# State-space output with channels on partitions, and decay exponents from four shared products with rows spread by small DMAs

## What is computed

```python
scores = einsum('bic,bjc->bij', q, q); out = softmax(scores) @ v * gamma + inputs        # attention over 1024 tokens
t = layernorm(out)                                                                      # then a state-space layer
dt = softplus(dt + dt_bias); dA = exp(dt * -exp(A_log))                                 # 8 heads
state = state * dA_t + (dt_t * x_t) * B_t;  y = einsum('bhpn,bn->bhp', state, C_t)      # 8 heads x 32 channels, 32 states
y = rmsnorm((y + Dp * xs) * silu(z), gnorm_w, 1e-05);  t = t + x + y @ W_out.T
logits = layernorm(t) @ router_w.T                                                      # then 8 experts, the best 2 per token
```

## Time and profile before

| | |
|---|---|
| median of 3 runs | 1214.97 us (1214.96 to 1219.69) |
| span of the profiled execution | 1181.1 us |
| median minus span | 33.9 us |
| busy share of the span: PE, DVE, ACT, POOL | 92%, 72%, 64%, 53% |
| mean granted TensorE clock | 0.970 |

### The profile page before, as it was taken

One profiled execution on the slowest core, in us unless ns is written; L12 is line 12 of the kernel. 1 busy time (PEld: TensorE's weight loads), 2 busy tenths in 40 slices (PEclk: granted clock), 3 DMA queues, 4 the chain that ended last, 5 costly groups with the idle time before them and its releaser, 6 DMA issues.

```text
span 1181.1 us, 29643 instructions
## 1 busy us (share of the span) xinstructions
PE 1083.7 (92%) x8432; PEld 998.3 (85%) x8433; DVE 852.1 (72%) x3071; ACT 754.7 (64%) x1903; POOL 624.9 (53%) x981
## 2 busy tenths in 40 slices
PE   3889999999999999999999999867889999999993
PEld 2779888888988988988888888856789999999883
DVE  3488888988988888888898898776355644444564
ACT  1567777777767777767777777742476666666551
POOL 8122444467557566556646655743744665444442
PEclk9999999999999999999999999976799999999997
DMA  7200000001000100100100000010122222223666
GB/s 221 61 1 28 10 2 28 6 24 39 11 25 11 38 19 18 39 20 10 46 6 24 22 13 15 10 28 10 49 60 62 80 78 74 73 64 92 173 181 183
DMA packets 76439, 57.73 MB, mean 49 GB/s; under 512 B 10725, under 2 KB 70669, under 8 KB 76301
## 3 DMA queue, kind: packets, MB, share of 16 engines
q1 hardware_dynamic: 58285, 33.75, 10.5%
q0 software_dynamic: 8704, 17.97, 4.5%
q10 hardware_dynamic: 9312, 4.33, 1.3%
HBM read 32.27 MB, written 24.81 MB: 48 GB/s over the span
## 4 chain that ended last, share of the span: by engine, by line
PE 60%; DVE 11%; POOL 10%; issue 10%; ACT 3%; DMA 2%; SPq 2%; DVEq 1%; POOLq 0%; ACTq 0%
PE pc L433 7%; PE pY L588 7%; PE pX L583 6%; PE pa L483 5%; PE pb L600 3%; PE pd L600 3%; PE pY L399 3%; DVE CV L1232 2%; PE pc L437 2%; POOL rows_by_expert L991 2%; PE pX L412 2%; PE pa L444 2%; PE pX L414 2%; PE pX L413 2%; DMA GX<-rows_by_expert 2%
## 5 line engine op out<-in xcount | busy, mean ns | idle before, releaser
L1003 POOL DMA_INDIRECT results_by_choice<-YE,DIX x144 | 143.2, 995 | 147.6 <-ACT YE L786 132.5
L991 POOL DMA_INDIRECT rows_by_expert<-XA,SL x128 | 147.6, 1153 | 35.2 <-issue 35.2
L1481 DVE TENSOR_TENSOR V<-XT,pY 128x384 f32<-128x384 f32 x144 | 79.7, 554 | 116.1 <-ACT XT L777 111.5
L433 PEld LDWEIGHTS pc<-XDT,M 128*128 128x128 f32 x1024 | 128.3, 198 | 14.0 <-issue 9.5
L433 PE MATMUL pc<-XDT,M 128*128 128x64 f32 x1024 | 126.6, 279 | 6.4 <-DVE CT L1238 6.4
L1232 DVE SCALAR_TENSOR_TENSOR CV<-XBC,cw,CV 128x256 f32<-128x256 f32 x288 | 132.0, 513 | 0.0
L483 PE MATMUL pa<-V,PT 128*128 128x128 f32 x1024 | 127.3, 278 | 0.2 <-issue 0.2
L934 POOL TENSOR_TENSOR YG<-Y,SZ 128x256 f32<-128x256 f32 x64 | 46.5, 726 | 149.5 <-DVE Y L1266 135.7
L583 PE MATMUL pX<-TA,XBC 128*128 128x128 f32 (+1 forms) x864 | 121.2, 277 | 2.3 <-ACT TA L769 1.9
L588 PE MATMUL pY<-TA,XBC 128*128 128x128 f32 (+1 forms) x864 | 121.2, 277 | 1.2 <-DVE XBC L1485 1.0
L483 PEld LDWEIGHTS pa<-V,PT 128*128 128x128 f32 x1024 | 119.3, 192 | 2.7 <-issue 0.7
(11 more groups left out here) (283 smaller groups left out, 2891.6 us busy)
## 6 DMA issues: line engine op xcount, KB each, us to landing
GX<-rows_by_expert SPq DMA_DIRECT2D x144, 65.0 KB, 1.8
XT<-in_xT_dram SPq DMA_DIRECT2D x8, 512.0 KB, 4.0
X<-in_x_dram SPq DMA_DIRECT2D x16, 256.0 KB, 3.0
out_dram<-T ACTq DMA_DIRECT2D x16, 256.0 KB
results_by_choice<-YE,DIX POOLq DMA_INDIRECT x144
rows_by_expert<-XA,SL POOLq DMA_INDIRECT x128, 2.4
XA<-results_by_choice SPq DMA_DIRECT2D x8, 256.0 KB, 5.1
W<-in_w1T_dram SPq DMA_DIRECT2D x1, 1364.0 KB
```

What stands on the lines that cost most here:

```text
L433: mm(pc[:, 64 * h:64 * h + 64], M[:, h, :], XDT[:, e % 2, HD * h:HD * h + 64], start=h == 0, stop=False, skip_group_check=True)
L991: g.indirect_dma_start(xg, bass.IndirectOffsetOnAxis(ap=SL[:, j // NT, j % NT:j % NT + 1], axis=0), XA[:, j // NT, j % NT, :], None).then_ ...
L1003: g.indirect_dma_start(yg, bass.IndirectOffsetOnAxis(ap=DIX[:, j, :], axis=0), YE[:, j, :], None).then_inc(s(f"ye{j}_scattered"), 16)
L1481: tt(HT[:, par].rearrange("p k t -> p (k t)"), SH[:, par, :], pY[:, 512 * par:512 * par + HP3], ALU.mult).then_inc(s("hh_ready"), 1)
```

## The change

- **Output with channels on partitions.** `YO`, `Y2`, `YG`, `SZ` hold channels on partitions and tokens along a row. In L433 the weights are now 32 columns of `XDT` and `M` (128 columns) moves; the result of head `h` goes to 32 partitions of `pc`, those of group `h % 4`. The skip term and the product of state and C (L551) swap their operands in the same way, the `z` projection too, with `dt` and router columns as a second product.
- **No transposes of the output.** `YG` feeds the output projection as it is. L467 and the copy `YT` go. The sum of squares, which was ACT's accumulator, is now: `SQ` on ACT, an add of its two halves on POOL (`SQS`), a product with ones on PE into `pb` behind the output projection, `RY` on ACT from `pb`, and the root on POOL.
- **Router part and result in one DVE instruction** of 136 columns into `T2X`; `LR` and `XR` go.
- **Decay by token.** `ECUM` goes; `ECT` is the exponential of a 128 x 256 product of `pickc` and `CT3` (two bf16 products, one ACT instruction).
- **Exponents from four products.** `RX` holds on rows 0 to 47 the pattern and on rows 48 to 95 the cumulated decays themselves, one row for each part and head; rows 96 on hold a mask. Four bf16 products `NCT3[q]` by `RX`, of 256 columns each, give all exponents. The rows 48 to 95 are written by 16 DMAs from `CT3` for every two tiles, 3 partitions of 256 bytes each, issued by SP behind `ct3_ready`; PE waits for `cum_rows`.

```diff
+            def spread(base, i):
+                if there(base, i - 5):
+                    if base + i == 5:
+                        sp.wait_ge(s("masks"), 1)
+                    sp.wait_ge(s("ct3_ready"), base + i - 3)
+                    for h2 in range(2 * H):
+                        sp.dma_start(RX[48 + h2:96:2 * H, h2, :], CT3[h2:48:2 * H, (i - 5) // 2 % 2, :]).then_inc(s("cum_rows"), 16)
...
-                    mm(pb[:, 0:DI + H + E], XNT[:, 0:P], wz[:], start=True, stop=True).then_inc(s("z_ps"), 1)
+                    mm(pb[:, 0:2 * P], wz[:, 0:P], XNT[:], start=True, stop=True, skip_group_check=True)
+                    mm(pb[:, 2 * P:2 * P + H + E], XNT[:, 0:P], wz[:, DI:], start=True, stop=True, skip_group_check=True).then_inc(s("z_ps"), 1)
...
                     for h in range(H):
-                        mm(pc[:, 64 * h:64 * h + 64], M[:, h, :], XDT[:, e % 2, HD * h:HD * h + 64], start=h == 0, stop=False, skip_group_check=True)
+                        m, rows = h // 4, slice(HD * (h % 4), HD * (h % 4) + HD)
+                        mm(pc[rows, P * m:P * m + P], XDT[:, e % 2, HD * h:HD * h + HD], M[:, h, :], start=m == 0, stop=False, skip_group_check=True)
...
-                    for h2 in range(2):
-                        four = pY[:, 512 * h2:512 * h2 + 512].rearrange("p (h t) -> p h t", h=4)
-                        for th in range(2):
-                            mm(four[:, :, HP * th:HP * th + HP], NCT3[:, par, th, :], pickm[:, half * H + 4 * h2:half * H + 4 * h2 + 4, :], start=th == 0, stop=False, skip_group_check=True)
-                    for h in range(H):
-                        last = mm(pY[:, P * h:P * h + P], pick[:, half * H + h, :], CT3[:, par, :], start=False, stop=True, skip_group_check=True)
+                    pe.wait_ge(s("cum_rows"), 16 * 2 * H * ((base + k) // 2 + 1))
+                    for q_ in range(4):
+                        last = mm(pY[:, H * QT * q_:H * QT * q_ + H * QT], NCT3[:, par, q_, :], RX[:, half * H:half * H + H, QT * q_:QT * q_ + QT], start=True, stop=True, skip_group_check=True)
                     last.then_inc(s("d_ps"), 1)
-                if there(base, e):
-                    upto(pe, "yg_ready", base, e + 1)
+                    for m in range(2):
+                        last = mm(pd[:, 2 * P + P * m:3 * P + P * m], pickc[:, half * H + 4 * m:half * H + 4 * m + 4, :].rearrange("p h d -> p (h d)"), CT3[:, par, :], start=True, stop=True, skip_group_check=True)
+                    last.then_inc(s("ect_ps"), 1)
...
-                        last = nc.tensor.transpose(pb[:, P * m:P * m + P], YG[:, P * m:P * m + P], ident[:])
-                    last.then_inc(s("yT_ps"), 1)
...
-                        last = mm(pb[:, 0:C + E], YT[:, m, :], wo[:, m, :], start=m == 0, stop=m == 1)
+                        last = mm(pb[:, 0:C + E], YG[:, m, :], wo[:, m, :], start=m == 0, stop=m == 1, skip_group_check=True)
                     last.then_inc(s("out_ps"), 1)
+                    upto(pe, "sqs_ready", base, e + 1)
+                    mm(pb[:, C + 2 * E:C + 2 * E + 2], SQS[:], ones[:, 0:2], start=True, stop=True, skip_group_check=True).then_inc(s("ss_ps"), 1)
...
-                    A(ECUM[:, dpar], CT[:, 0], ACT.Exp)
...
-                    A(SQ[:], YG[:], ACT.Square, accum_out=SS[:]).then_inc(s("ss_ready"), 1)
+                    A(SQ[:], YG[:].rearrange("p m t -> p (m t)"), ACT.Square).then_inc(s("sq_ready"), 1)
...
-                    A(YT[:].rearrange("p a b -> p (a b)"), pb[:, 0:DI], ACT.Copy).then_inc(s("yT_ready"), 1)
+                    A(ECT[:].rearrange("p m t -> p (m t)"), pd[:, 2 * P:4 * P], ACT.Exp).then_inc(s("ect_ready"), 1)
...
-                    A(NCT3[0:48, dpar], pd[:, :].bitcast(bf16)[0:48, None, 0:P].broadcast_to([48, 2, P]), ACT.Copy, scale=-1.0).then_inc(s("ct3_ready"), 2)
+                    A(NCT3[0:48, dpar], pd[:, :].bitcast(bf16)[0:48, None, 0:P].broadcast_to([48, 4, P]), ACT.Copy, scale=-1.0).then_inc(s("ct3_ready"), 2)
...
+                    A(RY[:, 0, 0:1], pb[:, C + 2 * E:C + 2 * E + 1], ACT.Identity, bias=epsc[:], scale=1.0 / DI).then_inc(s("sst_ready"), 1)
...
+                    g.tensor_tensor(SQS[:], SQ[:, 0:P], SQ[:, P:2 * P], ALU.add).then_inc(s("sqs_ready"), 1)
+                    upto(pool, "sst_ready", base, e + 1)
                     upto(pool, "t2_ready", base, e)
-                    g.tensor_scalar(RY[:, 0, 0:1], SS[:], 1.0 / DI, RMS_EPS, ALU.mult, ALU.add).then_inc(s("sst_ready"), 1)
...
-                    stt(LR[:, e % NT, :], pb[:, C:C + E], RY[:, 1, 0:1], XR[:, e % NT, :], ALU.mult, ALU.add)
+                    stt(T2X[:, base + e, :], pb[:, 0:C + E], RY[:, 1, 0:1], TRX[:, e % NT, :], ALU.mult, ALU.add).then_inc(s("t2_ready"), 1)
...
-                    stt(t2, pb[:, 0:C], RY[:, 1, 0:1], TR[:, e % NT, :], ALU.mult, ALU.add).then_inc(s("t2_ready"), 1)
```

156 lines of the change are left out of this document (85 added, 71 removed).

## The result

The changed kernel takes 1384.13 us (median of 4 executions, 1381.65 to 1385.23) against 1215.36 us for the kernel before (4 executions, 1214.96 to 1219.69): ratio 1.138, 95% interval 1.136 to 1.140. It is 169 us slower where 16 us less were forecast, and it lies outside the range.

A forecast was written before the change was run, and what follows sets the result against it. PE's own work, 98% busy, was taken to bound the kernel before; after the change, a loop through the DMA wait: 8.8 + 14.4 + 0.2 = 23.4 us a pair, -0.5 over 31 pairs, -16 us from 1214.97: 1199 us, range 1150 to 1236.

The forecast's parts named there:

- The new wait: PE before L457 of even steps waits for SP's 16 DMAs; closed loop, pair 23.4 us against 23.92, -0.5.
- D: Time from ct3_ready until the 16 DMAs have landed: 8.8 us, bounds 6.0 and 10.4.
- Rival 3: Slower by the DMA chain: interval 0.55 and landing 2.1 give +1.1 us a pair, 1249 us; chance 0.13.
- the rest of the way: From L457 of the even step to the next ct3_ready: 15.85 us before, 14.4 forecast, plus 0.2 in the sum.
- PE's saving: PE's work in a pair of tiles falls by 2.0 us, if nothing new is waited for.
- rival 2: Column groups of L433 overlap fully while the DMAs limit: -1.1 us a pair, 1181 us; chance 0.10.
- Passes of one head must follow each other: In L433 only a head's second pass overlaps the next head's first: 1.04 us, -0.70 a tile.
- The root: RY moves behind the output projection, reaching DVE near 539.2: 0 to 0.6 us a pair, 0 taken.
- rival 5: Late RY holds DVE and with it ST: +0.6 us a pair, near no change, 1216 us; chance 0.06.

The follow-up runs named there:

- warm_wait: Changed kernel with 14 useless products of 512 bf16 columns on PE ahead of the wait for the small DMAs in every even step: 1335.21 us.
- old_exponents: Changed kernel with the exponents made as in the kernel before, without RX and the small DMAs; new layout and column groups stay: 1230.43 us.
- two_hops: Changed kernel with the 16 DMAs of a pair replaced by three into an HBM array and one back: 1230.13 us.
- one_group: `old_exponents` with all heads' decay products writing the same 32 output partitions, one after another: 1245.68 us.
- gt_before_pr: `old_exponents` with DVE's third tap behind XDT, ACT's BNAT and GT ahead of PR (odd steps), PE's NCT products ahead of the transposes (even steps): 1235.20 us.
- no_root: `old_exponents` without the root of the mean square (no SQS, its product or RY; T2X scaled by one): 1205.20 us.
- sq_direct: `old_exponents` with the halves of SQ added by two products on PE in place of POOL's sum SQS: 1223.06 us.
- gt_early: `old_exponents` with ACT copying BNAT and GT ahead of the exponential PR in odd steps: 1231.72 us.

## Why the prediction was wrong

**The step that failed** is "The new wait", and in it D. Its form held: the loop is closed, PE waits before the exponents of the even steps for a DMA (32 times), and the pair is D plus the rest. Its size didn't: 0.682 us from issue to issue for 0.475, so 12.0 us for 8.8. The upper bound of 10.4 was too low as well. I took the interval from two small loads back to back and bounded it at 0.55, with a note that three rows might make an issue cheaper than any in the trace; it was dearer than most of them. The threshold for "slower" that the prediction names, D = 9.3, was 0.5 us away from my value, less than what I didn't know about the interval. The chances of the cases should have said so. Rival 3 had the mechanism and 1249 us. By the prediction's own sum, D = 12.0 gives 12.0 + 14.6 = 26.6 us a pair, +2.7 on 23.92, some 1298 us. So of the 5.9 us by which the pair of 29.3 us exceeds the forecast of 23.4, D has 3.2; the other 2.7 are in the rest of the way.

**The rest of the way** was forecast at 14.6 us and is 29.32 - 12.0 = 17.3. Its parts:
- The clock, absent from the prediction: 29.32 - 27.87 = 1.45 us a pair (`warm_wait`), 49 us measured on the time. It is at least that, since the clock of `warm_wait` is still 0.97. The stretch with chains of small operations had shown a clock of 0.70 when PE waits a lot, and the sum had no term for it. It makes a wait dearer than its length.
- The other 1.3 us are what the layout costs outside PE. The rows show waits for XDT, CTP and the mean square in the changed kernel as in `old_exponents`; that these are the 1.3 us, and how they add up beside the DMA wait, wasn't measured.

**The 169 us in one line.** 1384 to 1335: the clock, as far as the useless products give it back. 1335 to 1230: the queue of issues. 1230 to 1215: the layout. The first two are one cause, the wait for sixteen issues.

**PE's saving** was forecast at 2.0 us a pair. Busy times of 21.9 (`old_exponents`) and 0.860 x 24.66 = 21.2 us a pair (`two_hops`, with the new exponents) against 23.5 before show 1.6 and 2.3 us. So it is there, and the size was about right, but by luck: its largest part was mis-sized, L433 at 1.04 us measured 0.57, close to the 0.46 of rival 2, which makes 0.9 us a pair more; the other parts together saved some 0.6 us less than forecast (2.3 for 2.9), and which of them was not looked into. "Passes of one head must follow each other" was wrong reasoning. The Trainium skill (TensorEngine Tiling, Performance Considerations) lists the swap as a fourfold tiling, and the trace agrees: 0.57 us for 1.86. A cost of changing the mode isn't visible; in these rows it could hide only in the 0.1 us between 0.46 and 0.57.

**That the saving is time** was the second failure: it was made part of the rest of the way, pair by pair. PE at 98% was taken to mean that DVE and ACT have slack where PE gets shorter. `one_group` shows that it isn't so: 2.3 us of PE's work for 0.5 us of time. The explanation is argued from the rows and only in part tested. L433 and the transposes of YG stand between the scores and the attention output, where the rows of DVE and ACT that start at the scores need 3.3 us and PE had 4.1. By that, of 1.1 us saved there in an odd step, 0.8 could count at most. `two_hops` fits: its further saving reappears as a wait for XDT. But taking these waits away (`gt_before_pr`) gained nothing as long as the path of the root was long.

**The root**, rival 5, was costed at 0 for DVE, with "POOL comes just in time for YG". In the changed kernel DVE waits for it, 24.0 us in 200 to 900 us:

```profile
DVE T2X L1414 <- POOL RY L976: 24.0, 21, 1.7
```

That is 1.0 us a pair, more than rival 5's 0.6; what it costs there wasn't measured. In `old_exponents` it is some 0.15 us before each T2X (4.9 us in 32), POOL waits 4.3 us a pair, the sum SQS makes PE wait 0.4, and without the root the time is 25 us less (`no_root`). The step looked at the one reader of RY and neither at the root's own work nor at what stands behind the waiting instruction on POOL.

**Right**: the issues' load on the chip is harmless (0.3%), SP's other loads don't suffer (X 0.37 to 0.38 us to issue, for 0.37), `fill_up` isn't seen (410 us from the last C3 transpose to the end, for 402 to 411 in three variants of the kernel before), and the start is the same within 1 us (first C3 transpose at 63.9 us for 62.9).

The Trainium skill (DMA: Bandwidth & Descriptors, Anatomy of one DMA) gives 50 ns for the dispatch and 2 us fixed, for transfers that GpSimd issues. These are issued by SP, so the prediction had no right to hold its figures against the trace. The landing is near the 2 us even so (1.62 us from the start of the last issue, 1.0 from its end); the issue is 0.64 us in the trace, over ten times the 50 ns, and that decides this case.

What stays open: which of the root's own work, POOL's late root, its late scatters and the wait for SQS carries how much of the 25 us; `sq_direct` removes one hop and gets 7 us, the rest was only removed as a whole, and never in the kernel before. And `no_root` changes the router's choices, so its expert part, where 5 of the 25 us lie, needn't be the same; its pair of 23.81 us is read ahead of that part.

## What to carry to other kernels

Count the DMA issues between a producer and its consumer and multiply by the interval of such an issue, measured for that shape; the bytes don't matter at 0.8 KB, and four issues by way of HBM beat sixteen inside SBUF. An engine that is 98% busy says only that the others are hidden under it, not by how much (2.3 us of its work were worth 0.5 us here): before a saving is counted, measure at its very place how much longer the covering work is than the chain under it. That is a bound, not the price: here the moves against these waits brought nothing alone, one hop less for the root 7 us, both together 16. When a result moves later, look at everything that stands behind its readers on their engines. And price idle time of TensorE with the slow clock that may follow it; waits of up to 1.8 us in `old_exponents` left it at 1.00 on average, those before L478, 3.1 us in the mean (40.9 us in 13), did not.

## What was unexpected of the hardware

- A DMA of three rows of 256 bytes from SBUF to SBUF takes 639 to 827 ns to issue on SP, median 640, and 0.682 us from one to the next, at work (512 of them) and as idle load alike. DMAs of 16 rows from SBUF to HBM took 302, 420 and 842 ns (minimum, median, maximum), one of 48 rows from HBM to SBUF 302.
- 16 fp32 passes of 128 columns in four column groups of 32 take 0.57 us from start to start, where 16 full passes take 1.86, with the two passes of a head right behind each other.
- After PE had been idle for 3.0 us and, 0.8 us of work later, for 2.0 us, the granted clock was 0.50 from 542.7 to 547.5 us (the 16 attention products 3.72 us for 2.02). Fourteen products with no use in each even step made the kernel 3.5% faster.
- VectorE's small cast of C (128 x 16) takes 0.16 us on average in the kernel before, but 0.69 in `old_exponents` and 0.82 in `gt_early`. In one of the long ones (1.08 us from 250.52 in `old_exponents`) POOL is at work beside it; that this is the cause was not tested.
